# Pooled-keys attention: the first running sum moves in front of the barrier, a table is loaded early, and x is summed by TensorE

## The reference

```python
h = _layer_norm(hidden_states, gamma, beta)
keys = jnp.einsum('bsd,ed->bse', h, Wk) + bk
values = jnp.einsum('bsd,ed->bse', h, Wv) + bv
key_att = jnp.einsum('bsd,ed->bse', keys, Wka) + bka
keys_weight = jnp.exp(key_att / jnp.sqrt(jnp.asarray(d_model, h.dtype)))
keys_weight = keys_weight / jnp.cumsum(keys_weight, axis=1)
pooled_keys = jnp.cumsum(keys_weight * keys, axis=1)
return pooled_keys * values
```

## Time and profile before

| | |
|---|---|
| median of three runs | 1829.59 us |
| the profiled execution | 1828.96 us, its span 1826.9 us |
| mean granted TensorE clock | 0.904 of full |
| busy over the span | PE 1554.0 us (85%), DVE 1235.8 (68%), ACT 1029.2 (56%), POOL 592.3 (32%) |
| the stage of the change, barrier to barrier | 774.96 to 818.48 us, 43.5 us or 2.4% of the span |

### The profile page before, as it was taken

How to read it: one execution, slowest core, us unless ns; L and a number is a source line. 1 busy time by engine, 2 the same in 40 slices (tenths; PEclk the granted TensorE clock), 3 DMA queues, 4 the chain that set the end, 5 groups by cost and what they waited for, 6 DMA issues and landing times. The chain is left out here.

```text
span 1826.9 us, 25673 instructions
## 1 busy us (share of the span) xinstructions
PE 1554.0 (85%) x9076; PEld 1065.2 (58%) x9076; DVE 1235.8 (68%) x2893; ACT 1029.2 (56%) x1862; POOL 592.3 (32%) x630
## 2 busy tenths in 40 slices
PE   4998699998699699849998977997796699997696
PEld 3777233333477578627877965896695222223596
DVE  5687589884688744373535956595785589894686
ACT  2653378787455355345537732774375378885374
POOL 3675200001387301123116634664434200001533
PEclk9999689999799899969998988898798689999798
DMA  3121533400221220001000000000663643300465
GB/s 111 48 71 31 109 48 53 53 1 1 63 87 39 70 88 0 1 16 32 1 1 11 1 1 1 1 1 1 162 200 103 146 71 53 53 1 1 129 199 155
DMA packets 99510, 101.07 MB, mean 55 GB/s; under 512 B 22960, under 2 KB 82904, under 8 KB 99097
## 3 DMA queue, kind: packets, MB, share of 16 engines
q1 hardware_dynamic: 96439, 93.39, 21.7%
q0 software_dynamic: 2944, 6.05, 0.9%
HBM read 87.60 MB, written 15.78 MB: 57 GB/s over the span
## 5 line engine op out<-in xcount | busy, mean ns | idle before, releaser
L2574 DVE TENSOR_REDUCE mx<-bank 128x1 f32<-128x512 f32 (+1 forms) x512 | 318.0, 679 | 63.7 <-PE bank L2359 63.6
L2507 ACT ACTIVATE e<-bank 128x512 f32<-128x512 f32 x512 | 267.1, 602 | 61.6 <-PE bank L2389 60.7
L2389 PE MATMUL bank<-qq,kk 99*128 99x512 bf16 (+1 forms) x512 | 163.8, 396 | 5.3 <-ACT e L2507 5.3
L1539 POOL TENSOR_TENSOR midl<-mid,midh 128x512 fp32r<-128x512 f32 (+1 forms) x96 | 126.2, 1319 | 77.8 <-ACT midh L1459 77.5
L2640 POOL TENSOR_TENSOR osb<-ot,rc 128x128 f32<-128x128 f32 x32 | 13.0, 407 | 425.5 <-DVE rc L2599 425.5
L2389 PEld LDWEIGHTS bank<-qq,kk 99*128 99x128 bf16 (+1 forms) x512 | 39.8, 99 | 162.9 <-ACT e L2507 136.6
L1044 DVE TENSOR_TENSOR hl<-q,hh 128x512 fp32r<-128x512 f32 x64 | 45.9, 718 | 125.0 <-ACT hh L1014 103.1
L93 PE MATMUL bank<-wdh,midh 128*128 128x256 f32 (+1 forms) x384 | 112.3, 292 | 9.6 <-DVE x L1523 9.6
L185 PE MATMUL bank<-cf,xn 128*128 128x128 f32 x192 | 42.4, 364 | 83.1 <-ACT xn L248 40.5
L94 PE MATMUL bank<-wdl,midh 128*128 128x256 f32 (+1 forms) x384 | 110.2, 287 | 0.0
L95 PE MATMUL bank<-wdh,midl 128*128 128x256 f32 (+1 forms) x384 | 109.4, 285 | 0.0
(11 more groups left out here) (400 smaller groups left out, 4535.0 us busy)
## 6 DMA issues: line engine op xcount, KB each, us to landing
w<-in_L_ffn_W SPq DMA_DIRECT2D x30, 512.0 KB
w<-in_L_ffn_W SPq DMA_DIRECT2D x30, 256.0 KB
qq<-scratch SPq DMA_DIRECT2D x18, 384.0 KB
w<-in_L_ffn_w_kernel SPq DMA_DIRECT2D x16, 344.0 KB
w<-in_L_ffn_w_kernel SPq DMA_DIRECT2D x16, 320.0 KB
wo<-in_L_ffn_wo_kernel SPq DMA_DIRECT2D x16, 320.0 KB
sorted<-in_unsorted SPq DMA_DIRECT2D x2, 1935.0 KB, 11.2
g<-sorted SPq DMA_DIRECT2D x30, 129.0 KB, 2.3
```

The costliest lines, as they stand in the source:

```text
L1539: e.tensor_tensor(l[0:fn, o], mid[i % 2][0:fn, o], h[0:fn, o].bitcast(F32), ALU.subtract).then_inc(*l2_m_lo.tick(n, i, f))
L2389: e.matmul(b_bank(t, u, j), keys(kk[0:K], t, b)[:, k * 128:(k + 1) * 128], queries(qq[0:K], t, b), start=True, stop=True).then_inc(*at_b.t ...
L2507: e.activation(er[u][:, j * 512:(j + 1) * 512], b_bank(t, u, j), ACT.Exp, bias=0.0, scale=scale).then_inc(*at_e.tick(n, t, u, j))
L2574: e.tensor_reduce(mxa[t % 3][:, o:o + nkb], bank[place_a["a", t, u, j]].rearrange("p (k n) -> p k n", k=nkb), X, ALU.max).then_inc(*at_max ...
```

## The change

1. VectorE does the first two instructions of chunk 0 (running sum of kw and its reciprocal) in front of the barrier: a new hook `closing_dve` of `Pre` is called at the end of `begin_dve`. cum becomes four tensors of 512 columns, of which the first belongs to `Pre`.
2. ScalarE does an exponential of one column, whose result nobody reads, ahead of `turn_act(0)`, so that the exponential's table is loaded there.
3. In `add` TensorE no longer transposes pr alone (four transposes). It does per chunk eight matmuls in float32: four put x itself (identity times the x tile) into the bank, four add the transposed pr (pr against the identity). ScalarE then copies the bank over x (`put`), and VectorE's addition (L1254) is gone; its statistics wait for the copy. ScalarE does put(0) behind the chain of chunk 2, put(1) behind that of chunk 3, put(2) ahead of `finish_act(2)`, put(3) ahead of `finish_act(3)`. The bank's next user waits for the copy instead of the addition.

```diff
-        def begin_dve(q, m):
+        def begin_dve(q, m, pre):
             norm_dve(q, m, 3)
+            pre.closing_dve(q)
...
             def act(q):
+                q.wait_ge(*pre_in[m % 2].at(m))
+                q.e.activation(exp_table, cols[:, 0:1], ACT.Exp, bias=0.0)
                 turn_act(q, 0)
                 project_act(q, 0)
...
+            def weight_sums(q, c):
+
+                s = slice(c * 512, (c + 1) * 512)
+                q.wait_ge(*key_set.at("w", c))
+                q.e.tensor_tensor_scan(cum[c], cF("onesrow"), kw[:, s], 0.0, ALU.mult, ALU.add).then_inc(*step.tick())
+                q.wait_ge(*step.now())
+                q.e.reciprocal(cum[c], cum[c]).then_inc(*step.tick("sums", c))
+
+            def closing_dve(q):
+                weight_sums(q, 0)
...
                     for j in range(4):
-                        a = transpose(q.e, p[:, j * 128:(j + 1) * 128], pr[:, c * 512 + j * 128:c * 512 + (j + 1) * 128])
-                    a.then_inc(*back_turn.tick(c))
+                        q.e.matmul(p[:, j * 128:(j + 1) * 128], ident, x[:, 4 * c + j, :], start=True, stop=False)
+                        a = q.e.matmul(p[:, j * 128:(j + 1) * 128], pr[:, c * 512 + j * 128:c * 512 + (j + 1) * 128], ident, start=False, stop=True)
+                    a.then_inc(*back_sum.tick(c))
...
             def act(q):
+                def put(c):
+                    q.wait_ge(*back_sum.at(c))
+                    q.e.copy(x[:, 4 * c:4 * c + 4, :].rearrange("p t n -> p (t n)"), bank[place["o", c]]).then_inc(*x_put.tick("o", c))
+                    q.wait_ge(*x_put.now())
+
                 for c in range(CHUNKS):
                     if c + 1 < CHUNKS:
                         turn_act(q, c + 1)
                         project_act(q, c + 1)
                     if c > 0:
+                        put(c - 1)
                         finish_act(q, m, c - 1, stage, nxt)
+                put(CHUNKS - 1)
                 finish_act(q, m, CHUNKS - 1, stage, nxt)
...
                 def add(c):
-                    xc = x[:, 4 * c:4 * c + 4, :].rearrange("p t n -> p (t n)")
-                    q.wait_ge(*back_turn.at(c))
-                    e.tensor_tensor(xc, xc, bank[place["o", c]], ALU.add).then_inc(*xsum.tick(m, c))
-                    finish_dve(q, m, c, nxt)
+                    finish_dve(q, m, c, nxt, ready=x_put.at("o", c))
```

More of the change, by code:

```diff
@@ L76, with __init__ @@
 class Pre:
-    def __init__(self, sp, buf, pe=None, act=None, dve=None, pool=None, late=None, issue=None, route=None, early=None, halve_act=None, halve_pool=None, loaded=None):
+    def __init__(self, sp, buf, pe=None, act=None, dve=None, pool=None, late=None, issue=None, route=None, early=None, halve_act=None, halve_pool=None, loaded=None, closing_dve=None):
         nothing = lambda q: None
@@ L83, in __init__ @@
         self.early, self.halve_act, self.halve_pool = (f or none for f in (early, halve_act, halve_pool))
-        self.pe, self.act, self.dve, self.pool, self.late, self.issue = (f or nothing for f in (pe, act, dve, pool, late, issue))
+        self.pe, self.act, self.dve, self.pool, self.late, self.issue, self.closing_dve = (f or nothing for f in (pe, act, dve, pool, late, issue, closing_dve))
 def turns(uses, n):
@@ L1111, in build @@
         w4_turn, w4_xt, key_mm, key_set = (signal(n) for n in ("w4_turn", "w4_xt", "key_mm", "key_set"))
-        kk_set, pool_set, back_turn = signal("kk_set"), signal("pool_set"), signal("back_turn")
+        kk_set, pool_set, back_sum, x_put = signal("kk_set"), signal("pool_set"), signal("back_sum"), signal("x_put")
         def pre_l1_attn(m):
@@ L1116, in pre_l1_attn @@
             vals, kw, kk = (take(s, 2048) for s in ("vals", "kw", "kk"))
+            cum = [take("cum", 512)]
+            exp_table = take("exp", 1)
             keys = [take("keys", 512) for _ in range(2)]
@@ L1134, in claim @@
                 if b:
-                    q.wait_ge(*{"x": w4_xt, "k": key_set, "v": key_set, "w": key_set, "o": xsum}[b[0]].at(
-                        *((m + 1, b[1]) if b[0] == "o" else b)))
+                    q.wait_ge(*{"x": w4_xt, "k": key_set, "v": key_set, "w": key_set, "o": x_put}[b[0]].at(*b))
                 return bank[place[use]]
@@ L1193, in dve @@
                 q.e.tensor_scalar(cols[:, 3:4], cols[:, 3:4], 128 ** -0.5, None, ALU.mult).then_inc(*step.tick("bias"))
+            def weight_sums(q, c):
[6 more added lines that the diff above has]
+                weight_sums(q, 0)
             def pool(q):
                 project_pool(q, 0)
-            return Pre(sp, (cols, vals, kw, kk, place, claim, turn_pe, turn_act, project_pe, project_act, project_pool),
-                       pe=pe, act=act, dve=dve, pool=pool)
+            return Pre(sp, (vals, kw, kk, cum, place, claim, turn_pe, turn_act, project_pe, project_act, project_pool, weight_sums),
+                       pe=pe, act=act, dve=dve, pool=pool, closing_dve=closing_dve)
         def l1_attn(n, pre, prepare):
             m = n + 1
-            cols, vals, kw, kk, place, claim, turn_pe, turn_act, project_pe, project_act, project_pool = pre.buf
-            cum, pr = take("cum", 2048), take("pr", 2048)
+            vals, kw, kk, cum, place, claim, turn_pe, turn_act, project_pe, project_act, project_pool, weight_sums = pre.buf
+            pr = take("pr", 2048)
+            cum += [take("cum", 512) for _ in range(3)]
             nxt = prepare(m)
@@ L1238, in pool_keys @@
                     s = slice(c * 512, (c + 1) * 512)
-                    q.wait_ge(*key_set.at("w", c))
-                    e.tensor_tensor_scan(cum[:, s], ones, kw[:, s], 0.0, ALU.mult, ALU.add).then_inc(*step.tick())
+                    if c > 0:
+                        weight_sums(q, c)
+                    q.wait_ge(*step.at("sums", c))
+                    q.wait_ge(*kk_set.at(c))
+                    e.tensor_tensor(kk[:, s], kk[:, s], cum[c], ALU.mult).then_inc(*step.tick())
                     q.wait_ge(*step.now())
-                    e.reciprocal(cum[:, s], cum[:, s]).then_inc(*step.tick())
+                    e.tensor_tensor_scan(cum[c], ones, kk[:, s], 0.0, ALU.mult, ALU.add).then_inc(*step.tick())
                     q.wait_ge(*step.now())
[L1244 to L1249, removed]
+                    e.tensor_tensor(pr[:, s], cum[c], vals[:, s], ALU.mult).then_inc(*pool_set.tick(c))
                 def add(c):
-                    xc = x[:, 4 * c:4 * c + 4, :].rearrange("p t n -> p (t n)")
-                    q.wait_ge(*back_turn.at(c))
-                    e.tensor_tensor(xc, xc, bank[place["o", c]], ALU.add).then_inc(*xsum.tick(m, c))
-                    finish_dve(q, m, c, nxt)
+                    finish_dve(q, m, c, nxt, ready=x_put.at("o", c))
                 for c in range(CHUNKS):
@@ L2803, in dve_program @@
                 finish_dve(q, 0, c, first_pre, ready=x_in[c].at())
-            begin_dve(q, 0)
+            begin_dve(q, 0, first_pre)
             barrier(q, 0)
@@ L2808, in dve_program @@
                 if n + 1 < LAST:
-                    begin_dve(q, n + 1)
+                    begin_dve(q, n + 1, nxt)
                     barrier(q, n + 1)
```

## The result

| | before | changed |
|---|---|---|
| median of 19 runs | 1830.23 us (1827.97 to 1832.18) | 1833.66 us (1830.79 to 1840.66) |
| ratio, 95% | | 1.0021 [1.0015, 1.0028] |

The account below looks back on a forecast made before the run. Bounds: the wait ending last at the barrier (projection, table load, kw, kk), then chunk 1's chain, then VectorE. +2.6 - 1.38 + 1.77 = +3.0 us on 1829.59 gives 1832.6, 8 in 10 within 1830.0 to 1834.6.

Parts of the forecast that it names:

- Barrier: Barrier ahead of chunk 1's chain: early sum and reciprocal make VectorE last, delaying the release by +2.6 us.
- the two cases: At the barrier: sum ahead of kk, 2.1 us later; kk ahead, sum stretched, 3.1 us later; the middle was taken.
- Chain: Behind the barrier, chunk 1's turn, projections, xT, keys and kw: still 7.43 us, starting 2.6 us later.
- the sign that the prediction gave for it: Sign for rival 2: kw of chunk 1 comes more than 8.1 us behind the barrier.
- rival 2: Chunk 1's chain: TensorE idles longer, its clock rises one projection later; +4.0 us in all, 1833.6; 26%.
- The counterargument in the prediction: Against rival 2, in chunk 1's chain: same work from the same half clock should find the rise at the same distance.
- Additions: Additions of chunks 0 and 1 leave VectorE while it is the bound, their copies hidden: -1.38 us.
- End: From last pr to chunk 3's statistics: eight half-clock matmuls plus copy take 4.29 us against 2.52, +1.77 us.
- rival 1: Last chunk: TensorE has full clock at its last add, end costs +0.1; +1.3 us in all, 1830.9; 14%.
- Rival 4: Last chunk: a product costs four transposes, 9.0 us instead of 3.61; +8.4 us, 1838.0; 3%.
- Rival 3: TensorE keeps full clock over the barrier, chunk 1's chain some 2 us less; +1.0 us, 1828.9 to 1830.6; 5%.
- rival 5: Behind the barrier VectorE goes straight from chunk 0 to chunk 1, the change pays; -2.2 us, 1827.4; 4%.

Follow-up runs that it names:

- e1: Changed kernel with the first running sum and reciprocal back behind the barrier; 0.9996 of the kernel before, -0.7 us.
- e2: Kernel before with only the early running sum and reciprocal, no early table, x added by VectorE; 1.0013 of the kernel before, +2.4 us.
- e7: Changed kernel with chunk 1's turn, projections, xT, keys, vals and kw also in front of the barrier; 1.0002 of the kernel before, +0.4 us.
- e8: e7 with the last chunk's four transposes and its addition back on VectorE; 0.9984 of the kernel before, -2.9 us.
- e5: Changed kernel with the last chunk's four products of x ahead of TensorE's wait for pr; 1.0006 of the kernel before, +1.1 us.
- e9: e1 with the last chunk's four transposes and its addition back on VectorE; 0.9984 of the kernel before, -2.9 us.
- e12: Changed kernel with 12 bfloat16 products into an unused bank behind chunk 0's projections; 1.0019 of the kernel before, +3.5 us.
- e3: Kernel before with only the exponential's table loaded in advance; 0.9992 of the kernel before, -1.5 us.
- e4: Kernel before with only x summed by TensorE and copied by ScalarE; 0.9994 of the kernel before, -1.1 us.
- e6: Changed kernel with 24 bfloat16 products into an unused bank behind chunk 0's projections; 1.0019 of the kernel before, +3.5 us.

## Why the prediction was right, and where its numbers were off

- **Barrier, forecast +2.6 (+2.1 to +3.1): +2.0.** The mechanism held: the last drain is VectorE's, and e1 and e2 show that the early sum moves it. It fell as in the lower of the two cases (+2.1): sum and kk start 0.01 us apart (775.67, 775.66), too close to call one the first, and it is kk that is stretched. The middle, which the prediction took, is a value that neither case has.
- **Chain, forecast 7.43 us to the end of kw, as before, wherever it starts: 8.16** (788.50 - 780.34; 8.19 to the start of the sum). This is the step that was off in size. By the sign that the prediction gave for it, kw more than 8.1 us behind the barrier, rival 2 is what happened, with +0.7 of its +1.0. The clock is still 0.50 at 784 to 786, and 0.62 at 786 to 788, so it rose some 7.2 us behind the barrier; before, some 5.7. The counterargument in the prediction (same work from the same half clock) did not hold. Nor do the other profiles bear out the reason that rival 2 gave, TensorE's longer idle time ahead of the barrier: the table below has them.
- **Additions, -1.38: -1.44,** and within 0.02 us the same in every kernel whose adds left VectorE, but for e7 and e8 (23.42 and 23.53), which have the second source named under e7. The copies were in time: no statistics of chunks 0 to 2 wait for them.
- **End, +1.77: +1.98.** 4.50 us against 4.29 forecast, of which the products are 3.79 against 3.61. The half clock was there, so the fast end (rival 1) did not come. Against the rule of the Trainium skill weighed in the prediction (TensorE: Matmul & The Clock Gate, § Terms), the changed kernel has 3.79 us for eight products and before 1.12 for four transposes, both at half clock: 0.47 against 0.28 us a piece, 1.7 times and not 4. Rival 4, which needed 9.0 us, is refuted. e5, e8 and e9 confirm the place: 2.2 (partly at full clock) and 1.9 us when the work behind pr is less.
- **Rival 3** (the clock kept over the barrier) did not occur in either profile of the changed kernel, and **rival 5** was refuted by the 5.35 us of idle time.
- **What was missed.** All of the prediction stood on a profile with half clock in chunk 0. At full clock kk meets the norm and not the sum. Comparing like with like there, the early sum costs 12.63 - 8.13 = 4.5 us of the barrier (e12, e3) and not the 11.74 - 8.39 = 3.35 of half clock. An estimate for the whole change at full clock: e12's 57.56 against before's 54.05 - (9.76 - 8.37) = 52.7, so +4.9 us; with the chains that e4 and e3 have at full clock (7.80, 8.07) in place of 7.46 it is +4.6 or +4.3. The timed +3.8 lies between +3.1 and these. What share of the executions has which clock no run tells.

The chain and the clock in seven profiles, in us. The idle time is TensorE's ahead of its first transposes behind the barrier; how long the clock was half from the barrier to the end of the chain is worked out from the mean clock of stretches of 2 us, as above.

| kernel | idle | half clock | chain |
|---|---|---|---|
| 24 idle products (e6) | 1.4 | 0 | 5.49 |
| before | 3.5 | 5.7 | 7.46 |
| x first (e5) | 8.0 | 6.2 | 7.70 |
| late sum, last add on VectorE (e9) | 2.2 | 6.8 | 8.04 |
| table alone (e3) | 3.5 | 6.8 | 8.07 |
| early sum alone (e2) | 7.0 | 7.0 | 8.09 |
| changed | 5.6 | 7.2 | 8.19 |

The chain follows the time at half clock, and that time doesn't follow the idle time: e9 idles less than the kernel before and has a longer chain, e5 idles longest and has a shorter one than the changed kernel. The +0.7 us is shown to come with the later rise of the clock; what sets the moment of that rise stays open.

The sum came to +3.1 in the profiles, for +3.0 forecast, by errors that cancel (barrier -0.6, chain +0.7, end +0.2), which is luck rather than precision. The median 1833.66 is 1.1 above the forecast: outside the forecast's own 1832.1 to 1833.1, where rival 2 has its 1833.6, and inside the 8 in 10. 0.6 of that is the median of before, 1830.23 here against the 1829.59 on which the forecast stood.

## What to carry to other kernels

Work pulled in front of a barrier helps only the engine that does it. When that engine thereby becomes the last to arrive, everything behind the barrier pays the whole shift, so look first which chain starts there, and whether it or the moved work's engine ends last. Taking work from a busy engine gains in the middle of a stage, and loses at its end, where nothing is left to hide the slower substitute: change the chunks that are hidden and leave the last one (e9). And read a second execution at another clock before trusting which of two operations gets to a shared resource first.

## What the runs showed of the hardware

- Where an operation of GpSimd and one of VectorE (a running sum, a product or the norm) overlapped, one of the two was stretched, mostly the one that started later. The norm goes from 1.11 to 2.03 us (e12), VectorE's product from 0.69 to 1.70 (e7), the running sum of kk from 1.22 to 2.17 (before), GpSimd's kk from 1.26 to 2.28 (changed). In e12 kk is 0.09 us ahead and the norm gives way; in the changed kernel the two start within 0.01 us, and kk gives way. The reciprocal took 3.35 us beside kk as without it.
- The same chain behind the same barrier took 5.49 us with the clock full, 7.46 with it half for 5.7 us, and 8.04 to 8.19 with it half for 6.8 to 7.2. How long TensorE had idled ahead of the barrier (2.2 to 8.0 us) did not order them.
- The clock falls again between the chunks of the changed kernel (0.65 at 804 to 806; before, 0.58 at 794 to 796), although each of its adds keeps TensorE busy for longer than the four transposes did.
